# Reordering the end of the first attention and the shared expert's third group in a two-layer gated cross-attention and mixture kernel

## The chip, the cores and the metric

The kernel runs on one core of one Trainium2 chip. The metric is the device time in microseconds (us) of one execution. PE is the matmul engine (TensorE), PEld its weight loads, DVE the vector engine, ACT the scalar engine, POOL the GpSimd engine and SP the engine that issues most transfers. "SPq" and "ACTq" are transfers issued from those engines' queues.

## The reference

The input `x` is 16 batches of 128 rows by 256. Four layers follow one another, each added to `x` through a tanh gate:

```python
x = x + tanh(g_xattn[0]) * L0_xattn(layernorm(x), ctx)   # 16 heads, projections Wq Wk Wv Wo
x = x + tanh(g_ffn[0])   * L0_ffn(layernorm(x))          # 32 routed experts, top 4, CAP 128, and a shared expert
x = x + tanh(g_xattn[1]) * L1_xattn(layernorm(x), ctx, ctx)   # 8 heads
x = x + tanh(g_ffn[1])   * L1_ffn(layernorm(x))          # 8 experts, top 2, and a shared expert

# L0_ffn: sigmoid scores, the 4 best of 8 groups of experts, the 4 best experts in them
routed = sum over the 4 experts of weight * down(relu(up(x))**2)
shared = relu(x @ shared_up.T)**2 @ shared_down.T        # hidden width 512
```

The change touches the end of `L0_xattn`, all of `L0_ffn`, and the start of `L1_xattn`.

## The kernel before, in words

The whole of `x` stays on the chip as the tile `X`. Each engine has one program, written out by hand, in which the order of the work is the order of the code; an engine that waits on a semaphore holds back all that is behind it in its program. Semaphore waits are written `w.wait_ge(semaphore, value)`.

**Attention.** `attention_pe` (L401 on), `attention_dve` (L555 on), `attention_act`, `attention_pool` (L240 on) and `attention_sp` (L183 on) each run steps `t`. Within a step the first layer counts heads `k` from 0 to 15 (on ACT `m` from 0 to 7, by pairs of heads). At step `t` batch `t` is in its exponentials, batch `t - 2` in its denominators and output, and so on, so the steps 16, 17 and 18 (`NB`, `NB + 1`, `NB + 2`) only drain the last batches. In a drained step, what is left on PE for batch b is: `denominators` (L512, at k == 12 of step b + 2), then on DVE `normalized` (L626, k == 13), then on PE `output` (L519, k == 15), then on ACT the scaling into `rd` (L355, first thing in step b + 3), then on POOL the addition to `X` (L276). For the last batch, 15, this happens in steps 17 and 18. Each engine's program calls a `meanwhile` hook at each k or m, behind the attention's own work of that k. By it the first feed-forward layer is started inside the attention's last steps.

**Start of the first feed-forward layer.** On DVE: per group of four batches the row statistics (`rows`, L1197; `statistics`, L1204 and L1207), on POOL the inverse roots (`roots`, L778), on DVE the normalized values `XN` (`normed_rows`, L1212). On PE: pairs of batches are transposed (`transposed`, L823), copied out as columns (on DVE L1232, the last ones on ACT L991), multiplied with the gate's weights into rows of logits for a group of four batches (`logit_rows`, L833), copied out (DVE L1236 or ACT L996), and transposed back (`logits`, L842). ACT takes sigmoids of eight batches at a time (`sigmoids`, L1000). `marks_dve` then finds the chosen experts for eight batches in a chain of small DVE instructions (L1088 to L1125), written as a generator, so that it can be run a piece at a time: its pieces are the sum with the bias (L1088), four maxima and minima (L1091 to L1094), three more (L1096 to L1098), two (L1100, L1101), the comparisons (L1104, L1106, L1108, L1110, one piece each), and the rest (L1112 to L1125). It runs once for batches 0 to 7 and once for 8 to 15.

**Between.** `ffn0_pe` runs the shared expert in 16 chunks `hidden` (L880; chunk n is up projection c = n mod 4 of group n // 4) and four groups `down` (L892). ACT follows with `relu_squared` (L975, L977) and `copied_out` (L1023). In between DVE counts places (`route_dve`, L1138 to L1187) and PE sums a table of token indices (`table`, L923, four parts, each after its DVE comparison L1173). When the table is read (L1177, L1178), POOL issues the 32 gathers of rows for the routed experts (L800, one indirect transfer per expert).

**Routed experts.** For expert x, PE transposes the gathered rows (L946), multiplies expert x - 1 up (L957) and x - 2 down (L965); ACT copies (L1051, L1056), DVE squares (L1315) and scales (L1321). SP stores each result to `ye` (L759) and reloads weights for the last experts (L762).

**Behind them.** `ffn0_pe_later` runs the last four chunks `hidden` and the last `down`. `ffn0_act_later` does the same on ACT; its last two `copied_out` stand in step t = -4, m == 2, of the second attention, ahead of the three QS transfers that ACT issues at m == 3 (L162). The second attention's five programs start behind a barrier (`all_done`, `stage`) to which each engine adds one. The operands of attention scores sit in four stacks of the tile `QS`. Each stack of the second attention needs a load of keys (L180) and two transfers of constant rows (`holes`, L2167). Stacks of batches 2 and 3 lie where the shared expert's input columns `XT0` are, so they can only be filled after the last `hidden`. In the kernel before SP does so at the end of `ffn0_sp`, ahead of the barrier, and PE waits for them there. POOL gathers the expert results (L297, 64 transfers, 4 per batch) in a fixed number per step, DVE adds them (`gathered`, L598 to L602), and POOL's root for a batch (L280) stands between two runs of gathers. DVE maxima of scores are L589, PE scores L425.

`shared_added` (L1291) adds four batches of the shared expert's result to X: groups 0 and 1 before the experts, group 2 at expert 16, group 3 in step 1 of the second attention.

Of the kernel before, what the change touches and what calls it, by code (L numbers as in the profile page):

```python
# [21 lines left out]
U = 4  # L22
# [37 lines left out]
class Layer:  # L60


    def __init__(self, name, H, R, sem, before=None, gathers=None, keys=None, kept=None):
# [44 lines left out]
        self.s0 = 0 if self.first else 2  # L108

# [73 lines left out]
def attention_sp(e, w, A, M, loads, behind_first=None):  # L183
# [4 lines left out]
    for t in A.steps():  # L188
# [20 lines left out]
        if within(b1):  # L209
            if not A.first and b1 >= U:  # L210

                w.wait_ge(A.st, A.NP * (b1 - U + 1))
                keys_loaded(e, A, M, b1)
            w.wait_ge(A.res2, b1 + 1)
            w.wait_ge(A.st, A.NP * (b1 - U + 1))
            for k in range(3 if b1 == 0 else 6):
                spread(e, A, M, b1, k)
                if k == 2 and within(b5) and A.first:
                    reciprocals()
            if b1 == 0 and behind_first:  # L220
                behind_first()
        elif within(b5) and not A.late(b5):
            reciprocals()
# [181 lines left out]
def attention_pe(e, w, A, M, meanwhile=lambda t, k: None):  # L405
# [71 lines left out]
    def keys_of(b):  # L477
        w.wait_ge(A.ldc[b % U], 16 * ((A.n0 + b) // U + 1))
# [253 lines left out]

def ffn0_sp(e, w, G, A, B, M, d):
# [14 lines left out]
    def stack_ready(b):  # L748

        for k in range(2):  # L750
            w.wait_ge(B.kept[k], 96 * NB // 2)
        w.wait_ge(B.kept[2], 32)
        keys_loaded(e, B, M, b)
        for got in holes(e, M, d, B.stack(b), second=True):
            got.then_inc(G.late, 16)

    for x in range(E0):
        w.wait_ge(G.ey, x + 1)
        e.dma_start(M["ye_d"][CAP * x:CAP * x + CAP, :], M["YE"][x % 4]).then_inc(G.sty[x % 4], 16)  # L759
        if x + PLACES < E0:  # L760
            w.wait_ge(G.ed, x + 1)
            e.dma_start(M["EW"][x], M["ew_d"][x + PLACES, :, :]).then_inc(G.again[x], 16)  # L762

        if x in (PLACES - 4, PLACES):
            w.wait_ge(G.ed, x)
            stack_ready((x - PLACES + 4) // 4)

    w.wait_ge(G.up, 4 * NGRP)
    for b in (2, 3):
        stack_ready(b)  # L770
# [4 lines left out]
def ffn0_pool_meanwhile(e, w, G, M):  # L775
    def roots(g):
        w.wait_ge(G.bn, 3 * g + 3)
        e.tensor_tensor(M["frs"][:, GB * g:GB * g + GB], M["fve"][:, GB * g:GB * g + GB], M["mhalf4"][:, :],  # L778
                        ALU.pow).then_inc(G.rs, 1)

    def at(t):
        if t == NB - 2:
            roots(0)
            roots(1)
        if t == NB - 1:
            roots(2)
        if t == NB + 2:
            roots(3)

    return at  # L790
# [15 lines left out]
def ffn0_pe_meanwhile(e, w, G, A, M):  # L806
# [20 lines left out]
    def logit_rows(g):  # L827
        w.wait_ge(G.xt, 2 * g + 2)
        w.wait_ge(G.lc, g)
        if g == 3:  # L830
            w.wait_ge(A.exp, A.NP * NB)
        for a in range(2):
            got = e.matmul(BK[5 if g == 3 else 1][0:E0, :], M["GW"][:, a, :], XT[:, a, 512 * g:512 * g + 512],  # L833
                           start=(a == 0), stop=(a == 1))
# [62 lines left out]
def ffn0_pe_later(e, w, G, M):  # L897

    w.wait_ge(G.er, E0)
    hidden(e, w, G, M, 12, 13, 14, 15)  # L900
    w.wait_ge(G.ey, E0)
    down(e, w, G, M, 3)
    w.wait_ge(G.xs, NB)
    w.wait_ge(G.late, 16 * (PLACES - EARLY + 2 * U))


def ffn0_pe(e, w, G, A, M):
# [30 lines left out]
    down(e, w, G, M, 2)  # L938
    w.wait_ge(M["w_e"], 16 * EARLY)
    w.wait_ge(G.late, 16 * (PLACES - EARLY))  # L940
    for x in range(E0 + 2):
# [19 lines left out]
        if 0 <= y < E0:  # L961
            w.wait_ge(G.es, y + 1)
            w.wait_ge(G.xs, NB - GB)
# [21 lines left out]
def ffn0_act_meanwhile(e, w, G, A, M):  # L985
# [17 lines left out]
    def at(t, m):  # L1003
        if t == NB + 1 and m == 0:
            sigmoids(0, 2)
        if t == NB + 2 and m == 7:
# [19 lines left out]
def ffn0_act_later(e, w, G, M):  # L1026

    relu_squared(e, w, G, M, 12, 13, 14, 15)
# [9 lines left out]
def ffn0_act(e, w, G, M):  # L1038
# [7 lines left out]
    copied_out(e, w, G, M, 8, 12)  # L1046
# [144 lines left out]
def ffn0_dve_meanwhile(e, w, G, A, M, step):  # L1191
# [8 lines left out]
    def statistics(g, last):  # L1200
        last.then_inc(G.bn, 1)
        w.wait_ge(G.bn, 3 * g + 1)
        for b in range(GB * g, GB * g + GB):
            got = e.bn_aggr(mv[:, b, :], M["f6"][:, b, :])  # L1204
        got.then_inc(G.bn, 1)
        w.wait_ge(G.bn, 3 * g + 2)
        e.tensor_scalar(M["fve"][:, GB * g:GB * g + GB], mv[:, GB * g:GB * g + GB, 1], EPS, None, ALU.add).then_inc(G.bn, 1)  # L1207

    def normed_rows(g):
        w.wait_ge(G.rs, g + 1)  # L1210
        for b in range(GB * g, GB * g + GB):
# [22 lines left out]
    def logit_rows(g):  # L1234
        w.wait_ge(G.lr, g + 1)
        e.tensor_copy(M["LR"][g % 2], M["BK"][1][0:E0, :]).then_inc(G.lc, 1)  # L1236
# [7 lines left out]
    def at(t, k):  # L1244
# [22 lines left out]
        if t == NB and k == 14:  # L1267
            logit_rows(0)
        if t == NB + 1:
            if k == 0:  # L1270
                logit_rows(1)
                columns(4, 5)
            if k == 15:
                rows(12, 15)
                marks(1)
        if t == NB + 2 and k == 15:
            statistics(3, rows(15, 16))
            marks(1)
            normed_rows(3)
            for _ in first:  # L1280
# [13 lines left out]
def ffn0_dve_later(e, w, G, M):  # L1294
    def at(t, k):
        if t == 1 and k == 6:
# [5 lines left out]
def ffn0_dve(e, w, G, A, M, step):  # L1302
# [6 lines left out]
    for x in range(E0 + 1):  # L1309
        if x == E0 // 2:  # L1310
            shared_added(e, w, G, M, 2)
# [55 lines left out]
SHARED = ((0, 128), (128, 128), (256, 96))  # L1367

# [802 lines left out]
def build(nc, d, out):  # L2171
    with ExitStack() as ctx:
# [42 lines left out]
        def sp_program(e):  # L2215
# [23 lines left out]
            attention_sp(e, w, L1, M, lambda e, w, n: rows(n))  # L2239
# [154 lines left out]
```

## Time and profile before

| what | value |
|---|---|
| median of 3 runs | 773.63 us (771.66 to 774.16) |
| the profiled execution, its own time | 771.27 us |
| its span in the trace | 769.5 us |
| busy, share of the span | PE 87%, PEld 45%, DVE 68%, ACT 48%, POOL 45% |
| mean granted TensorE clock | 0.959 |
| first attention ends, about | 264 us (last addition to X) |
| routed experts | 317 to 372 us |
| second attention's first scores | 394 us |

Times in the rows are us from the start of the span. A timeline row is: start, duration, engine, line, operation, output and inputs, shapes, count, and in brackets the idle time before it with what ended it. Rows with "x4" merge several instructions. An f32 matmul is two instructions in these rows. Matmul ends are modelled.

### The profile page before, as it was taken

Reading aid. Unit: us, or ns where it says so; the run is one execution under the profiler, and the core shown is the slowest. Engines: PE = TensorE matmul, PEld = TensorE weight load, DVE = VectorE, ACT = ScalarE, POOL = GpSimd, SP = SyncE. Lnnn points to the kernel's source line nnn. Section 1 sums busy time; section 2 is a strip of 40 time slices with the busy share of each in tenths; the row PEclk is TensorE's granted clock in tenths of the full one; section 3 lists DMA queues with packets and bytes.
Section 4 is the critical chain, followed back from the end, with each engine's and each line's share of the span. In section 5 each row is a group of like instructions: output and inputs, shape, how many; then the busy total and the mean of one; then the engine's idle time right before and its main releaser. Section 6 shows DMA issues by size and latency. Waiting matters only on the chain.

```text
span 769.5 us, 13735 instructions
## 1 busy us (share of the span) xinstructions
PE 668.0 (87%) x4737; PEld 347.7 (45%) x4738; DVE 523.1 (68%) x1248; ACT 368.9 (48%) x612; POOL 343.6 (45%) x401
## 2 busy tenths in 40 slices
PE   3889999999999999778845699999887999897996
PEld 1233333333333356667512344445332566565763
DVE  3788888898887599435267799998636832332336
ACT  2057777877778354234413566666402213333420
POOL 3836465564412100655367887520100067666530
PEclk9999999999999999979966999999969999999999
DMA  6945454565522660245644778877511022222137
GB/s 157 196 114 138 129 141 131 158 179 151 156 65 67 200 179 14 67 122 149 209 128 127 206 217 236 221 197 194 161 46 29 0 68 81 73 67 74 49 94 265
DMA packets 111708, 101.12 MB, mean 131 GB/s; under 512 B 26517, under 2 KB 95802, under 8 KB 111512
## 3 DMA queue, kind: packets, MB, share of 16 engines
q1 hardware_dynamic: 99872, 76.19, 35.4%
q0 software_dynamic: 8352, 18.74, 8.6%
q10 hardware_dynamic: 3416, 5.31, 2.8%
q8 instruction: 38, 0.62, 0.4%
q14 instruction: 30, 0.25, 0.1%
HBM read 58.49 MB, written 24.40 MB: 108 GB/s over the span
## 4 chain that ended last, share of the span: by engine, by line
PE 54%; DVE 17%; issue 9%; POOL 6%; DMA 5%; SPq 4%; another core or an unknown queue 2%; ACT 2%; ACTq 0%; POOLq 0%; DVEq 0%
PE S L425 9%; PE O L470 9%; PE ST L1537 5%; DVE mx L589 5%; POOL spare L297 3%; PE ST L433 3%; PE ST L1463 2%; PE M L1554 2%; PE S L1554 2%; PE M L519 2%; PE ST L957 2%; PE M L512 2%; SPq L174 2%; DMA QS<-mxT 1%
## 5 line engine op out<-in xcount | busy, mean ns | idle before, releaser
L589 DVE TENSOR_REDUCE mx<-S 128x2 f32<-128x512 f32 x384 | 250.9, 684 | 34.8 <-PE S L425 33.1
L345 ACT ACTIVATE PX<-ST 128x1024 f32<-128x1024 f32 x192 | 196.2, 1024 | 92.0 <-PE ST L433 84.6
L425 PE MATMUL S<-QS 62*128 62x256 bf16 (+1 forms) x768 | 150.7, 292 | 39.5 <-DVE mx L589 26.0
L433 PE MATMUL ST<-QS 64*128 64x256 bf16 (+1 forms) x768 | 140.0, 276 | 1.4 <-DMA QS<-mxT 1.1
L470 PE MATMUL O<-PX,VA 128*32 128x256 f32 x1536 | 122.3, 391 | 0.3 <-DMA VA<-in_val 0.2
L425 PEld LDWEIGHTS S<-QS 62*128 62x128 bf16 (+1 forms) x768 | 47.7, 97 | 157.4 <-DVE mx L589 95.3
L297 POOL DMA_INDIRECT spare<-ye,GI x64 | 67.7, 1058 | 29.1 <-DMA ye<-QKc 14.8
L1648 POOL DMA_INDIRECT PX<-xn,TI x39 | 39.9, 1022 | 63.6 <-DVE K1n L1837 39.7
L800 POOL DMA_INDIRECT PX<-xn,TI x32 | 34.5, 1077 | 58.7 <-DVE spare L1186 44.1
L433 PEld LDWEIGHTS ST<-QS 64*128 64x128 bf16 (+1 forms) x768 | 53.3, 96 | 16.1 <-issue 9.0
L1537 PE MATMUL ST<-EGU,Cb 128*128 x156 | 54.7, 474 | 4.7 <-issue 2.9
L1655 POOL DMA_INDIRECT yt<-QKc,DI x39 | 39.3, 1008 | 24.5 <-ACT QKc L1617 17.0
L276 POOL TENSOR_TENSOR X<-X,rd 128x256 f32<-128x256 f32 x16 | 11.6, 727 | 86.2 <-ACT rd L355 81.2
L470 PEld LDWEIGHTS O<-PX,VA 128*32 128x32 f32 x1536 | 30.4, 108 | 41.1 <-issue 39.1
L280 POOL TENSOR_TENSOR rs<-ve,mhalf 128x1 f32<-128x1 f32 x32 | 18.1, 565 | 50.7 <-DVE ve L581 50.0
L1537 PEld LDWEIGHTS ST<-EGU,Cb 128*128 128x128 f32 x156 | 27.1, 193 | 15.1 <-issue 7.0
L308 POOL TENSOR_TENSOR QKc<-QKc,QKs 128x512 f32<-128x512 f32 (+1 forms) x29 | 27.0, 929 | 13.5 <-ACT QKs L394 10.9
L1965 DVE TENSOR_TENSOR rd<-ST,rd 128x176 f32<-128x176 f32 x19 | 6.5, 342 | 37.8 <-ACT rd L1610 21.3
L1965 DVE TENSOR_TENSOR Xn<-ST,Xn 128x176 f32<-128x176 f32 x20 | 6.8, 342 | 35.7 <-ACT Xn L1610 28.5
L337 ACT ACTIVATE OS<-O 128x512 f32<-128x512 f32 x48 | 28.1, 585 | 2.3 <-DMA rd<-OS 1.9
L317 POOL TENSOR_TENSOR QKs<-QKc,QKs 128x512 bf16<-128x512 f32 (+1 forms) x29 | 27.4, 947 | 3.2 <-ACT QKs L397 1.6
L880 PE MATMUL ST<-QS,SU 128*128 128x512 f32 x64 | 28.7, 598 | 0.1
(302 smaller groups left out, 1127.3 us busy)
## 6 DMA issues: line engine op xcount, KB each, us to landing
QS<-QKs SPq DMA_DIRECT2D x93, 128.0 KB
QS<-keys SPq DMA_DIRECT2D x16, 512.0 KB
keys<-spare SPq DMA_DIRECT2D x96, 64.0 KB
QS<-QKs SPq DMA_DIRECT2D x93, 64.0 KB
EGU<-in_ew SPq DMA_DIRECT2D x16, 256.0 KB, 2.7
xn<-spare SPq DMA_DIRECT2D x8, 512.0 KB, 5.7
ye<-QKc SPq DMA_DIRECT2D x32, 128.0 KB
VA<-in_val SPq DMA_DIRECT2D x16, 256.0 KB
```

Of the source, the lines that this page charges most:

```text
L297: e.indirect_dma_start(out=M["GA"][b7 % 3][:, T * k:T * k + T], out_offset=None, in_=M["ye_d"], in_offset=bass.IndirectOffsetOnAxis(ap=M[" ...
L345: e.activation(M["PX"][pair % 4][:, :], M["ST"][pair % 2][:, :], ACT.Exp, scale=A.scale).then_inc(A.exp, 1)
L425: got = e.matmul(M["S"][n % 2][:, 256 * a:256 * a + 256], QS[:, 0, 128 * a:128 * a + 128], QS[:, 1, :], start=True, stop=True)
L433: got = e.matmul(M["ST"][(NP * t + k // 2) % 2][:, 512 * u + 256 * a:512 * u + 256 * a + 256], QS[:, 1, 128 * a:128 * a + 128], QS[:, 0, : ...
L470: got = e.matmul(M["O"][32 * u:32 * u + 32, 256 * (quad % 2):256 * (quad % 2) + 256], V[:, a, 4 * quad + u, :], M["PX"][pair % 4][:, 512 * ...
L589: e.tensor_reduce(M["mx"][b % 2][:, :, A.row_of_max(head)], M["S"][n % 2][:, :].rearrange("p (a s) -> p a s", a=2), AX.X, ALU.max, negate= ...
L800: e.indirect_dma_start(out=M["GX"][x % GATHERS], out_offset=None, in_=M["xn_d"], in_offset=bass.IndirectOffsetOnAxis(ap=M["TI"][:, x:x + 1 ...
L880: got = e.matmul(M["BK"][3 + n % 2], M["SU"][:, a, 128 * c:128 * c + 128], M["XT0"][:, a, 512 * g:512 * g + 512], start=(a == 0), stop=(a ...
L1537: got = e.matmul(BK[3 + 2 * (j % 2)][:, 0:2 * I1], M["XeT1"][j % 2][:, 128 * a:128 * a + 128], M["EGU"][:, bass.ds(expert[j], 1), a, :], s ...
L1554: got = e.matmul(BK[1 if j % 2 else 7][:, 0:T], M["HT1"][j % 2][0:HALF, 128 * a:128 * a + 128], M["ED"][:, bass.ds(expert[j], 1), a, :], s ...
L1648: e.indirect_dma_start(out=M["XE1"][i % TILES], out_offset=None, in_=M["xn1_d"], in_offset=bass.IndirectOffsetOnAxis(ap=M["TI1"][:, i:i + ...
L1655: e.indirect_dma_start(out=M["yt_d"], out_offset=bass.IndirectOffsetOnAxis(ap=M["DI1"][:, j:j + 1], axis=0), in_=M["YE"][j % 4][:, :], in_ ...
```

## The change

On all five engines the steps 16 to 18 of the first attention are refilled, groups for the normalization become 4, 4, 4, 2, 2 batches (table `NORMS`), the third `down` goes from before the routed experts to behind them, and the last stacks of keys are loaded by SP behind the second attention's second spread (`b1 == 1`) where they were ahead of the barrier. PE's wait for them moves to the scores that use them (`holes`).

```diff
+        self.holes = 0 if self.first else 32
...
-            if b1 == 0 and behind_first:
+            if b1 == (0 if A.first else 1) and behind_first:
                 behind_first()
...
     def keys_of(b):
-        w.wait_ge(A.ldc[b % U], 16 * ((A.n0 + b) // U + 1))
+        w.wait_ge(A.ldc[b % U], 16 * ((A.n0 + b) // U + 1) + A.holes)
...
         if x in (PLACES - 4, PLACES):
             w.wait_ge(G.ed, x)
-            stack_ready((x - PLACES + 4) // 4)
-
-    w.wait_ge(G.up, 4 * NGRP)
-    for b in (2, 3):
-        stack_ready(b)
+            stack_ready(e, w, B, M, d, (x - PLACES + 4) // 4)
...
+        if t == NB + 1:
+            roots(3)
         if t == NB + 2:
-            roots(3)
+            roots(4)
...
+        if g % 2:
             w.wait_ge(A.exp, A.NP * NB)
         for a in range(2):
-            got = e.matmul(BK[5 if g == 3 else 1][0:E0, :], M["GW"][:, a, :], XT[:, a, 512 * g:512 * g + 512],
+            got = e.matmul(BK[5 if g % 2 else 1][0:E0, :], M["GW"][:, a, :], XT[:, a, 512 * g:512 * g + 512],
...
         if t == NB:
+            if k == 3:
+                logit_rows(0)
             if k == 12:
-                logit_rows(0)
+                logit_rows(1)
             if k == 15:
-                logit_rows(1)
                 logits(0)
+                logits(1)
                 transposed(4)
         if t == NB + 1:
             if k == 1:
-                logits(1)
                 transposed(5)
+            if k == 3:
+                logit_rows(2)
+            if k == 13:
+                hidden(e, w, G, M, 0)
             if k == 15:
-                logit_rows(2)
-                hidden(e, w, G, M, 0, 1)
+                transposed(6)
+                hidden(e, w, G, M, 1)
         if t == NB + 2 and k == 15:
-            transposed(6, 7)
+            transposed(7)
             logit_rows(3)
...
 def ffn0_pe_later(e, w, G, M):
     w.wait_ge(G.er, E0)
-    hidden(e, w, G, M, 12, 13, 14, 15)
+    hidden(e, w, G, M, 12, 13)
     w.wait_ge(G.ey, E0)
+    down(e, w, G, M, 2)
+    hidden(e, w, G, M, 14, 15)
     down(e, w, G, M, 3)
     w.wait_ge(G.xs, NB)
-    w.wait_ge(G.late, 16 * (PLACES - EARLY + 2 * U))
...
     for q in range(4):
         table(q)
-    down(e, w, G, M, 2)
...
+        if t == NB + 1 and m == 7:
             logit_rows(2)
             relu_squared(e, w, G, M, 0)
-            columns(6, 7)
+        if t == NB + 2 and m == 7:
+            columns(6)
             relu_squared(e, w, G, M, 1)
+            columns(7)
             logit_rows(3)
...
 def ffn0_act_later(e, w, G, M):
-    relu_squared(e, w, G, M, 12, 13, 14, 15)
+    relu_squared(e, w, G, M, 12, 13)
+    copied_out(e, w, G, M, 8, 12)
+    relu_squared(e, w, G, M, 14, 15)
     copied_out(e, w, G, M, 12, 14)
...
-        if t == NB and k == 14:
-            logit_rows(0)
+        if t == NB:
+            if k == 12:
+                logit_rows(0)
+            if k == 14:
+                logit_rows(1)
         if t == NB + 1:
-            if k == 0:
-                logit_rows(1)
+            if k == 1:
                 columns(4, 5)
+            if k == 2:
+                marks(4)
+            if k == 14:
+                statistics(3, rows(12, 14))
+                marks(1)
             if k == 15:
-                rows(12, 15)
+                rows(14, 15)
                 marks(1)
         if t == NB + 2 and k == 15:
-            statistics(3, rows(15, 16))
-            marks(1)
             normed_rows(3)
+            statistics(4, rows(15, 16))
+            marks(2)
+            normed_rows(4)
...
 def ffn0_dve_later(e, w, G, M):
     def at(t, k):
+        if t == -1 and k == 3:
+            shared_added(e, w, G, M, 2)
         if t == 1 and k == 6:
             shared_added(e, w, G, M, 3)
...
-        if x == E0 // 2:
-            shared_added(e, w, G, M, 2)
...
+NORMS = ((0, 4), (4, 8), (8, 12), (12, 14), (14, 16))
...
+            def columns_left():
+                w.wait_ge(X.up, 4 * NGRP)
+                for b in (2, 3):
+                    stack_ready(e, w, L1, M, d, b)
+
+            attention_sp(e, w, L1, M, lambda e, w, n: rows(n), columns_left)
```

## Rows read from the trace of the kernel before

**Rows 1.** Windows 262 to 267 us: busy of PE, PEld, DVE, ACT, POOL, then granted clock, DMA share, GB/s

```profile
262.00:267.00 5.00, 4.71 (x8) 1.38 (x9) 3.26 (x15) 1.06 (x2) 1.61 (x2) 0.66 1.02 334
```

**Rows 2.** Timeline of PE at the first attention's end

```profile
256.81 1.88 PE L833 MATMUL S<-QS,GW 128*32 128x512 f32 x4 [0.23 <-DVE QKc L1236]
...
260.42 0.66 PE L823 MATMUL S<-ident,spare 128*128 128x128 f32 x4 [0.42 <-DVE QS L1232]
...
261.00 0.69 PE L512 MATMUL M<-rT,hbL 16*128 16x256 f32 x2
...
262.29 1.19 PE L519 MATMUL M<-on,Wo 128*128 128x256 f32 x2 [0.59 <-DVE on L626]
...
263.41 3.06 PE L833 MATMUL S<-QS,GW 128*32 128x512 f32 x4
...
274.65 7.13 PE L880 MATMUL ST<-QS,SU 128*128 128x512 f32 x16
```

**Rows 3.** Timeline of DVE, same stretch

```profile
259.67 0.69 DVE L1232 COPY QS<-S 128x512 f32<-128x512 f32 x1 [0.27 <-PE S L823]
...
264.99 0.43 DVE L1197 BATCH_NORM_STATS2 f<-X 128x6 f32<-128x256 f32 x1 [1.45 <-POOL X L276]
...
267.39 1.38 DVE L1212 TENSOR_SCALAR spare<-X,fmv,frs 128x256 f32<-128x256 f32 x4 [0.61 <-POOL frs L778]
...
277.10 0.43 DVE L1088 TENSOR_TENSOR spare<-spare,bc 128x256 f32<-128x256 f32 x1
```

**Rows 4.** Timeline of ACT, same stretch

```profile
263.52 0.56 ACT L355 ACTIVATE rd<-M,bog,tg 128x256 f32<-128x256 f32 x1 [3.10 <-PE M L519]
...
269.04 0.63 ACT L977 ACTIVATE RL<-RL 128x512 f32<-128x512 f32 x1
...
274.76 0.38 ACT L1000 ACTIVATE spare<-ST 128x256 f32<-128x256 f32 x1 [0.52 <-PE ST L842]
```

**Rows 5.** Timeline of PE, the last quarter of the table

```profile
309.20 0.64 PE L923 MATMUL M<-OS,PX 128*128 128x64 bf16 x16 [1.13 <-DVE PX L1173]
```

**Rows 6.** Timeline of POOL: the second gather for the routed experts

```profile
312.97 1.92 POOL L800 DMA_INDIRECT PX<-xn,TI  x1 [0.31 <-issue]
```

**Rows 7.** Transfers, 310 to 320 us: GB/s in 40 slices of 0.25 us

```profile
GB/s 0 0 0 0 0 0 0 0 0 0 0 0 0 2 0 0 0 0 0 0 0 0 221 129 240 0 0 2 0 0 0 0 98 37 0 0 0 1 10 0
```

**Rows 8.** Timeline of PE, the end of the third down and the first expert

```profile
315.80 1.03 PE L892 MATMUL O<-SD,Cb 128*128 128x256 f32 x4
...
316.67 0.60 PE L946 MATMUL S<-ident,PX 128*128 128x128 f32 x4
```

**Rows 9.** The chain that ended last, 318 to 375 us: start, us, what

```profile
322.39 2.86 another core or an unknown queue
```

**Rows 10.** Timeline of PE behind the routed experts

```profile
372.21 7.13 PE L880 MATMUL ST<-QS,SU 128*128 128x512 f32 x16
...
380.78 1.97 PE L892 MATMUL ST<-SD,RL 128*128 128x256 f32 x8 [1.44 <-issue]
...
386.04 1.89 PE L892 MATMUL O<-SD,RL 128*128 128x256 f32 x8
...
393.95 1.01 PE L425 MATMUL S<-QS 126*128 126x256 bf16 x4 [6.03 <-DMA QS<-QKs]
```

**Rows 11.** Timeline of ACT behind the routed experts

```profile
384.51 0.47 ACT L1023 ACTIVATE spare<-O,tg 128x256 f32<-128x256 f32 x1 [1.25 <-PE O L892]
...
387.82 0.42 ACT L394 ACTIVATE QKs<-QKc 128x256 bf16<-128x256 f32 x1 [2.84 <-issue]
...
390.09 1.87 ACTq L162 DMA_DIRECT2D QS<-QKs  x3
```

**Rows 12.** Timelines of SP, DVE and POOL behind the routed experts

```profile
381.53 1.12 SPq L2167 DMA_DIRECT2D QS<-in_hole  x2
...
384.15 0.69 DVE L598 TENSOR_TENSOR spare<-spare 128x512 f32<-128x512 f32 x1 [11.53 <-issue]
...
399.81 0.56 POOL L280 TENSOR_TENSOR rs<-ve,mhalf 128x1 f32<-128x1 f32 x1 [2.25 <-DVE ve L581]
```

More of the change, by code:

```diff
@@ L730, in up_chunk, with stack_ready @@
     return n // 4, n % 4
+def stack_ready(e, w, B, M, d, b):
+    for k in range(2):
+        w.wait_ge(B.kept[k], 96 * NB // 2)
+    w.wait_ge(B.kept[2], 32)
+    keys_loaded(e, B, M, b)
+    for got in holes(e, M, d, B.stack(b), second=True):
+        got.then_inc(B.ldc[b % U], 16)
 def ffn0_sp(e, w, G, A, B, M, d):
@@ L746, in ffn0_sp @@
     e.dma_start(rows[:, :, T:ROW0], M["wd"]).then_inc(G.wrow, 16)
[L748 to L755, printed above, removed]
     for x in range(E0):
@@ L775, in ffn0_pool_meanwhile, with roots @@
 def ffn0_pool_meanwhile(e, w, G, M):
[L776 to L779, printed above, removed]
+    def roots(n):
+        lo, hi = NORMS[n]
+        w.wait_ge(G.bn, 3 * n + 3)
+        e.tensor_tensor(M["frs"][:, lo:hi], M["fve"][:, lo:hi], M["mhalf4"][:, 0:hi - lo], ALU.pow).then_inc(G.rs, 1)
     def at(t):
@@ L829, in logit_rows @@
         w.wait_ge(G.lc, g)
-        if g == 3:
+        if g % 2:
             w.wait_ge(A.exp, A.NP * NB)
         for a in range(2):
-            got = e.matmul(BK[5 if g == 3 else 1][0:E0, :], M["GW"][:, a, :], XT[:, a, 512 * g:512 * g + 512],
+            got = e.matmul(BK[5 if g % 2 else 1][0:E0, :], M["GW"][:, a, :], XT[:, a, 512 * g:512 * g + 512],
                            start=(a == 0), stop=(a == 1))
@@ L962, in ffn0_pe @@
             w.wait_ge(G.es, y + 1)
-            w.wait_ge(G.xs, NB - GB)
+            w.wait_ge(G.xs, NB - 2 * GB)
             w.wait_ge(G.ey, y - 1)
@@ L1005, in at @@
             sigmoids(0, 2)
-        if t == NB + 2 and m == 7:
+        if t == NB + 1 and m == 7:
             logit_rows(2)
             relu_squared(e, w, G, M, 0)
-            columns(6, 7)
+        if t == NB + 2 and m == 7:
+            columns(6)
             relu_squared(e, w, G, M, 1)
+            columns(7)
             logit_rows(3)
@@ L1045, in ffn0_act @@
     relu_squared(e, w, G, M, 10, 11)
-    copied_out(e, w, G, M, 8, 12)
     for x in range(E0 + 1):
@@ L1198, in rows, with statistics, normed_rows @@
         return got
-    def statistics(g, last):
+    def statistics(n, last):
+        lo, hi = NORMS[n]
         last.then_inc(G.bn, 1)
-        w.wait_ge(G.bn, 3 * g + 1)
-        for b in range(GB * g, GB * g + GB):
+        w.wait_ge(G.bn, 3 * n + 1)
+        for b in range(lo, hi):
             got = e.bn_aggr(mv[:, b, :], M["f6"][:, b, :])
         got.then_inc(G.bn, 1)
[L1206 to L1211, printed above, removed]
+        w.wait_ge(G.bn, 3 * n + 2)
+        e.tensor_scalar(M["fve"][:, lo:hi], mv[:, lo:hi, 1], EPS, None, ALU.add).then_inc(G.bn, 1)
+    def normed_rows(n):
+        w.wait_ge(G.rs, n + 1)
+        for b in range(*NORMS[n]):
             e.tensor_scalar(M["XN"][:, b, :], M["X"][:, b, :], mv[:, b, 0:1], M["frs"][:, b:b + 1],
@@ L1235, in logit_rows @@
         w.wait_ge(G.lr, g + 1)
-        e.tensor_copy(M["LR"][g % 2], M["BK"][1][0:E0, :]).then_inc(G.lc, 1)
+        e.tensor_copy(M["LR"][g % 2], M["BK"][5 if g % 2 else 1][0:E0, :]).then_inc(G.lc, 1)
     first = marks_dve(e, w, G, M, step, 0, 8)
@@ L2238, in sp_program @@
             rows = ffn1_sp_meanwhile(e, w, G1, M)
-            attention_sp(e, w, L1, M, lambda e, w, n: rows(n))
+            def columns_left():
[3 more added lines that the diff above has]
+            attention_sp(e, w, L1, M, lambda e, w, n: rows(n), columns_left)
             ffn1_sp(e, w, G1, M, o_out)
```

## The prediction

> **What bounds the kernel now.** I read the windows first, then the timelines of the engines over three stretches, then the chain that ended last. In the first stretch, 252 to 310 us, the chain goes from the last batch's output matmul on PE [rows 2] over its scaling on ACT [rows 4], the addition on POOL and the statistics on DVE (264.99 us) to the normalized values (267.39 us), and from there through DVE alone: the first marks, the second marks (from 277.10 us) [rows 3], the routing, up to the last quarter of the table, for which PE has waited 1.13 us [rows 5]. PE is thus only 1.13 us behind being the bound. In the second stretch, the experts, it is PE and ACT passing work on, with waits that the chain puts down to an unknown queue; the first is 2.86 us [rows 9] and the chain has four of them between 322.39 and 332.45 us. In the third, behind the experts, the chain runs over POOL's gathers, but each of POOL's roots has waited for DVE's statistics (2.25 us at 399.81 us) [rows 12], and DVE had to wait for the operands of the first scores, with PE, until 393.95 us [rows 10]. The reader is to see that DVE, not POOL's issue, sets the pace there.
>
> **The change, part by part.** Sums are made in the profiled execution (771.27 us, its span 769.5 us); it stands 2.36 us under the median of 773.63 us, and I add that at the end.
>
> **First logits earlier.** A row of logits is 1.88 us on PE [rows 2], copies on DVE 0.69 us [rows 3]. The first starts behind the last value matmuls at 253.5 us, its copy ends at 256.1 us, the second ends at 258.0 us. Then come output 14 (0.65), two sets of logits (0.36 each, the second behind its copy) and a pair's transposes (0.6 us, [rows 2]) up to 259.9 us. Copy, transposes, copy bring the columns of batches 8 to 11 at 262.0 us. Where the old PE program ran the last batch's denominators at 261.00 us [rows 2], the new one first runs the third row of logits, at full clock until 263.9 us. Denominators at 263.9 us, then `hidden(0)` (1.78 us, a fourth of 7.13 [rows 10]), then the output at 266.3 us, against 262.29 us [rows 2]. The old output took 1.19 us at a low clock; taking 0.65 us, it ends at 267.0 us.
>
> **Four marks ahead.** They are 0.45 + 0.85 + 0.77 + 0.5 = 2.6 us of DVE and fit where DVE would wait for the denominators, 262.0 to 264.6 us. They cost nothing as long as PE has that row of logits to run; without this cover they would delay the normalized values by 2.6 us.
>
> **The scaling.** ACT now has `relu_squared(0)` in front of the last scaling: relu and square, 0.63 us each [rows 4]. The scaling starts at 267.65 us against 263.52 us, and the last statistics at 269.1 us against 264.99 us: 4.1 us later.
>
> **What is given back.** Behind them DVE has two batches to aggregate and norm instead of four (0.7 for 1.38 us [rows 3]), the root on POOL lies under two marks, and all comparisons of the first marks are done. 269.1 + 0.45 statistics + 0.45 aggregation + 1.45 marks + 0.7 + 4.2 for the remaining marks gives 276.3 us. But the second marks wait for the second sigmoid: from the normalized values at 272.1 us transposes 0.6, columns 0.65, logits 1.88, copy 0.6, logits 0.36, sigmoid 0.4 with hand-overs lead to 276.8 us. Against 277.10 us [rows 3] DVE gains 0.3 us. PE starts `hidden(2)` at 276.35 us against 274.65 us [rows 2], 1.7 us later; of these 1.13 us vanish in its wait before the table [rows 5]. So the table, and with it all gathers, come **0.6 us later**; I keep 0 to 1 us with no change of clock.
>
> **The third down, taken out before the experts.** It is four times 1.73 us of PE, 6.9 us (from 380.78 to 386.04 us three of four [rows 10]). What hid it is the gathers: the second one was issued for 1.92 us from 312.97 us [rows 6], and its data moved from 315.5 to 316.25 us [rows 7], while PE came out of its down at 316.67 us [rows 8]. The second expert's transposes stand in front of the first up projection, so the loop can start only 0.4 us earlier. With gathers 0.6 us later the two cancel. Bounds: every later expert could be up to 1.2 us ahead, as the small gathers land about that much before they are used; and nothing is gained if the waits on the unknown queue [rows 9] have fixed ends. I take 0.2 us later, with 1.2 us earlier to 0.6 us later as bounds. The addition taken from DVE in the loop, 1.2 us, stood before a wait for a later expert, so it brings 0; at most 0.8 us, by which that expert was late. Put into step -1 it lies in a wait for a gather.
>
> **The third down, put behind them.** PE then has 6.9 us more before it starts the second attention. The `down`s are in order, so ACT's copy at 384.51 us [rows 11] comes at 391.4 us, and the ACT program has this copy in front of its first cast of the second attention: 387.82 us [rows 11] becomes 391.9 us, 4.1 us later. The last `down` ends at 387.93 + 6.9 = 394.85 us [rows 10]. The last two copies stand, on ACT, in front of the three QS transfers of batch 0. These go out at 395.4 us instead of 390.09 us [rows 11]; the first scores start at 399.3 us instead of 393.95 us [rows 10], **5.3 us later**. Queued behind on DVE are three maxima, the additions of batch 2 and its statistics; for these POOL's root waits (399.81 us [rows 12]), and behind it the next gathers. All move by 5.3 us. The lower bound is 4.1 us, should only the cast count; it is less only if POOL's schedule takes it up (a rival).
>
> **The key loads, moved.** SP ended them at 382.65 us, then took part in the barrier, and DVE started at 384.15 us with no transfer named as its releaser [rows 12]. Without them DVE can start about 2 us earlier, at gather speed; but ACT's cast at 391.9 us comes later than all of that. Price 0, bound -2 us. Behind the second spread they cost SP 3.3 us of issue, in front of a transfer for which SP waited 10 us: 0. The higher values in PE's waits cost nothing. The added transfers beside the gathers are a rival below.
>
> **Sum.** 0.2 + 5.3 = 5.5 us: 776.8 us in this execution, **779.1 us** as a median.
>
> **Rivals.**
>
> *Clock (0.15).* In 262 to 267 us the granted clock was 0.66 [rows 1], in part the level 1.2 GHz, after gaps of PE, and the row of logits took 3.06 instead of 1.88 us [rows 2]. If the new third row, the denominators and `hidden(0)` fall in such a stretch, 2.4 us are added in front of the output: 781.5 us. The new order has more and larger gaps from 258.6 to 262.0 us, about 1.4 of 3.4 us; against it, the old drop came before a dense stretch too. The Trainium skill ("TensorE: Matmul & The Clock Gate", Part 1) says that the throttled state is the default and activity releases it; by that rule, more gaps ahead of the row speak for this rival.
>
> *Keys beside gathers (0.12).* 1.3 MB for two stacks now move while POOL's gathers of batch 3 are under way, at 404 to 409 us. If these land 2 us later, DVE's additions and all behind do: 781 us. For it: between 381 and 383 us, while they ran, the 16 engines moved 342 GB/s and were full. Against it: the gathers there were in time. The Trainium skill ("DMA: Bandwidth & Descriptors", "Issuing engines are not separate DMA queues") says that SP's and POOL's transfers interleave on the same 16 engines, which supports it.
>
> *POOL takes it up (0.14, faster).* POOL needs 64 x 1.3 = 83 us for its gathers. If its issue sets the pace of the second attention's start, the roots' waits (2.25 us [rows 12] and four others) shrink, and the 5.3 us vanish there; the earlier barrier brings 2 us and the loop 1 us, less 0.6: 771.2 us. It decides if scores of batch 0 start no later than 396 us, or POOL shows no wait for them. Against it: in all five cases POOL was the one that waited.
>
> *The experts' waits shrink (0.17, no change).* Four waits of 9.4 us in sum hang on something that I can't name [rows 9]. With ACT and PE free at the loop's start they may fall by about half, 4.7 us: 774.4 us.
>
> *Forecast (0.42).* Its own range is 777 to 781 us.
>
> **How the numbers follow.** A measurement of this kernel can tell 0.3% (2.3 us) from no change, so the bounds are 771.3 and 775.95 us. Slower: forecast, clock and keys, 0.69. Same: the shrunk waits, 0.17. Faster: 0.14. The range goes from 773.5 us, inside the case of no change, to 783 us, which holds clock and keys with 1.5 us of spread.
>
> **What would show it.** Right: the last output matmul at 266 to 267 us, marks L1088 to L1101 in front of L626; second marks within 1 us of 277 us; no wait before the last quarter of the table; first expert within 1 us of 316.7 us; L880 and L892 in turn behind the experts up to 395 us; ACT's first cast near 392 us; the first L425 of the second attention near 399 us; POOL's root of batch 2 near 405 us. Wrong: first scores before 396 us, or the experts ending before 370 us.

## The result, and the profile after

In 20 runs each the kernel before took 769.97 us and the changed one 775.81 us, a ratio of **1.0092 [1.007, 1.0114]** (95% interval): slower. The medians lie 5.8 us apart, the ratio is worth 7.1 us (5.4 to 8.8). The two profiled executions differ by only 2.0 us (773.24 against 771.27), so places are compared in the traces and times by the ratio. The page of the changed kernel, its span and the shares of the chain that ended last:

```profile
span 771.4 us, 13739 instructions
...
PE 61%; DVE 12%; issue 9%; POOL 6%; DMA 4%; SPq 3%; ACT 2%; another core or an unknown queue 2%; ACTq 0%; POOLq 0%; DVEq 0%
```

In the chain of the kernel before PE had 54% and DVE 17%. In what follows, "cast" is ACT's L394 (L396 in the changed kernel), which turns a normalized batch of the second attention into bf16; the transfers of its operands (QS) go out behind it, and the first scores wait for them. "Root n" is POOL's root for batch n of the second attention.

**The first attention's end.** The timeline of PE in the changed kernel answers to [rows 2, 5]:

```profile
262.47 1.90 PE L834 MATMUL S<-QS,GW 128*32 128x512 f32 x4 [0.79 <-DVE QS L1243]
264.31 0.69 PE L514 MATMUL M<-rT,hbL 16*128 16x256 f32 x2
264.93 1.98 PE L887 MATMUL ST<-QS,SU 128*128 128x512 f32 x4
266.75 0.59 PE L521 MATMUL M<-on,Wo 128*128 128x256 f32 x2
...
276.65 7.13 PE L887 MATMUL ST<-QS,SU 128*128 128x512 f32 x16
...
308.51 2.03 PE L931 MATMUL M<-OS,PX 128*128 128x64 bf16 x64
```

Third row of logits, denominators, `hidden(0)` and last output stand in the order forecast; denominators and output start 0.4 and 0.45 us behind their forecast (263.9 and 266.3 us). The 64 products of the table now come in one piece: the 1.13 us of [rows 5] are gone. DVE's second marks answer to [rows 3]:

```profile
277.25 0.42 DVE L1098 TENSOR_TENSOR spare<-spare,bc 128x256 f32<-128x256 f32 x1 [0.62 <-ACT spare L1007]
```

277.25 against 277.10 us, and now it is the second sigmoid that they wait for, as forecast.

**The start of the experts.** PE's timeline answers to [rows 8]; the windows below it show the granted clock (third number from the right):

```profile
314.63 0.66 PE L953 MATMUL S<-ident,PX 128*128 128x128 f32 x2 [4.08 <-DMA PX<-xn,TI]
317.44 0.69 PE L953 MATMUL S<-ident,PX 128*128 128x128 f32 x2 [2.16 <-DMA PX<-xn,TI]
317.92 1.06 PE L964 MATMUL ST<-on,EGU 128*128 128x128 f32 x4
```

```profile
310.00:314.00 4.00, 0.54 (x19) 0.42 (x15) 3.14 (x10) 0.00 (x0) 1.61 (x2) 0.86 0.00 0
314.00:318.00 4.00, 1.22 (x5) 0.85 (x6) 0.70 (x1) 0.38 (x1) 3.39 (x3) 0.50 0.15 37
318.00:322.00 4.00, 4.00 (x19) 3.71 (x19) 1.07 (x3) 1.70 (x5) 3.08 (x4) 0.50 0.05 9
```

This I had not foreseen. Without the third down PE was busy for 1.76 of the 8 us from 310 to 318 us, the clock fell to 0.50 (1.2 GHz), and until 323 us each group of products of the up projection took 1.06 us instead of 0.61 to 0.71 us. The experts end at 374.1 us against 372.1 us.

**Behind the experts.** PE (answers to [rows 10]) and ACT (to [rows 11]):

```profile
384.66 3.60 PE L887 MATMUL ST<-QS,SU 128*128 128x512 f32 x8
389.60 1.99 PE L899 MATMUL ST<-SD,RL 128*128 128x256 f32 x8 [1.35 <-ACT RL L984]
...
394.88 1.89 PE L899 MATMUL O<-SD,RL 128*128 128x256 f32 x8
400.37 0.60 PE L427 MATMUL S<-QS 126*128 126x256 bf16 x4 [3.60 <-DMA QS<-QKs]
```

```profile
393.36 0.47 ACT L1032 ACTIVATE spare<-O,tg 128x256 f32<-128x256 f32 x1 [1.25 <-PE O L899]
393.73 0.41 ACT L396 ACTIVATE QKs<-QKc 128x256 bf16<-128x256 f32 x1
...
396.81 0.47 ACT L1032 ACTIVATE spare<-O,tg 128x256 f32<-128x256 f32 x1 [1.25 <-PE O L899]
396.82 1.87 ACTq L164 DMA_DIRECT2D QS<-QKs  x3
```

The cast stands directly behind the copy of the second of four downs, the three transfers directly behind the last copy; a cast that was ready earlier waited in ACT's program. DVE had the first batch normalized at 388.61 us (388.14 + 0.47), so the cast came 5.1 us after it could have; DVE's wait, 5.56 us, also holds the cast itself. Further on DVE waits for the gathers of batch 3 (timeline of DVE, the same row of the kernel before, then SP and POOL; to [rows 12]):

```profile
394.17 0.43 DVE L613 TENSOR_TENSOR QKc<-QKc,QKs 128x256 f32<-128x256 f32 x1 [5.56 <-ACT QKs L396]
...
412.82 0.69 DVE L600 TENSOR_TENSOR spare<-spare 128x512 f32<-128x512 f32 x1 [5.03 <-DMA spare<-ye,GI]
```

```profile
404.75 0.69 DVE L598 TENSOR_TENSOR spare<-spare 128x512 f32<-128x512 f32 x1 [2.91 <-DMA spare<-ye,GI]
```

```profile
404.40 0.59 SPq L182 DMA_DIRECT2D QS<-keys  x1
...
406.85 1.12 SPq L2189 DMA_DIRECT2D QS<-in_hole  x2
```

```profile
405.76 0.56 POOL L282 TENSOR_TENSOR rs<-ve,mhalf 128x1 f32<-128x1 f32 x1 [2.60 <-DVE ve L583]
406.50 1.05 POOL L299 DMA_INDIRECT spare<-ye,GI  x1 [0.18 <-issue]
407.85 1.00 POOL L299 DMA_INDIRECT spare<-ye,GI  x1 [0.30 <-issue]
...
415.86 0.56 POOL L282 TENSOR_TENSOR rs<-ve,mhalf 128x1 f32<-128x1 f32 x1 [3.24 <-DVE ve L583]
```

Root of batch 2 is 5.95 us behind 399.81 us [rows 12], that of batch 3 7.7 us behind its old place:

```profile
408.14 0.56 POOL L280 TENSOR_TENSOR rs<-ve,mhalf 128x1 f32<-128x1 f32 x1 [0.99 <-DVE ve L581]
```

The second pair of key loads went out beside the last two gathers of batch 3.

Root 15 is 8.5 us later in this pair (521.9 against 513.4 us), yet the spans differ by 1.9 us: from root 15 to the end the kernel before takes 256.1 us and the changed one 249.5 us, where nothing was changed. The twelve later profiles take 237.3 to 240.7 us there. So this pair's 2.0 us are no measure of the change, only the ratio is.

### The profile page after: what moved, and what is told of

Same layout as the page of the kernel before. It is cut to its first block, busy times and chain, and to the rows that moved or that the text cites. A ratio compares the mean times of both kernels' runs of the same rounds, so it can differ in the third digit from the quotient of the medians.

```text
span 771.4 us, 13739 instructions
## 1 busy us (share of the span) xinstructions
PE 667.1 (86%) x4738; PEld 350.6 (45%) x4738; DVE 523.9 (68%) x1249; ACT 368.7 (48%) x612; POOL 342.1 (44%) x402
## 4 chain that ended last, share of the span: by engine, by line
PE 61%; DVE 12%; issue 9%; POOL 6%; DMA 4%; SPq 3%; ACT 2%; another core or an unknown queue 2%; ACTq 0%; POOLq 0%; DVEq 0%
PE O L472 10%; PE S L427 10%; PE ST L1559 6%; DVE mx L591 5%; POOL spare L299 4%; PE ST L887 2%; PE ST L1485 2%; PE ST L435 2%; PE M L1576 2%; PE S L1576 2%; SPq L164 2%; PE M L521 2%; PE ST L964 2%; PE M L514 2%
## 5 line engine op out<-in xcount | busy, mean ns | idle before, releaser
L472 PEld LDWEIGHTS O<-PX,VA 128*32 128x32 f32 x1536 | 30.6, 108 | 41.9 <-issue 39.8
L310 POOL TENSOR_TENSOR QKc<-QKc,QKs 128x512 f32<-128x512 f32 (+1 forms) x29 | 27.0, 931 | 14.6 <-ACT QKs L396 12.6
```

Source lines behind the costliest of these rows:

```text
L472: got = e.matmul(M["O"][32 * u:32 * u + 32, 256 * (quad % 2):256 * (quad % 2) + 256], V[:, a, 4 * quad + u, :], M["PX"][pair % 4][:, 512 * ...
```

## The experiments

My theory was that the loss sits in ACT's order behind the experts; the rivals were the refill, the key loads beside the gathers, the clock at the loop's start, and PE's own time. In the three comparisons that follow the kernel before took 742.6 to 744.6 us, not 769.97; ratios are against the runs of before in the same comparison.

**One part at a time.** e1 has the diff's hunks for `ffn0_pe_meanwhile`, `ffn0_act_meanwhile`, the roots and DVE's statistics and marks alone. e2 has all the others. e3 has only the moved loads, e4 only the moved down, with ACT's copies and DVE's addition of it:

```
 e3: ffn0_sp            -    w.wait_ge(G.up, 4 * NGRP)
                        -    for b in (2, 3): stack_ready(b)
     attention_sp       +    behind_first() once b1 == 1
 e4: ffn0_pe            -    down(e, w, G, M, 2)
     ffn0_pe_later      +    down(e, w, G, M, 2)  between hidden(12, 13) and hidden(14, 15)
 e2: e3 and e4
```

> The kernel before with only the first attention's end changed (four marks ahead, the last group normed in two halves, the third row of logits and hidden(0) ahead of the last output). Theory: this part is worth 0.3 to 0.7 us, since the 4 us by which the last output comes later are given back at the second marks; ratio to the kernel before 1.000 to 1.001, second marks within 0.5 us of where the changed kernel has them (277.25 us), first expert at or before 317 us and no half-clock experts, since the third down still fills PE there. Rival (the whole loss lies in the refill, by way of a later table): ratio 1.007 or more.

> The kernel before with the third shared result behind the routed experts and the key loads behind the spread, the first attention's end as before. Theory: it has the whole loss, ratio 1.006 to 1.009 (+4.6 to +7 us), experts ending about 2 us later, first scores of the second attention about 6 us later. Rival (refill): ratio within 0.002 of one.

> The kernel before with the loads of keys and holes for two stacks behind the spread of the first batch, all else as before. Theory: the experts end as before; the additions behind them start about 2 us earlier, ACT's cast and the first scores with them (392 us for 393.95), but the transfers meet the gathers of batch 3, which costs about 2 us there: ratio 0.997 to 1.001. Rival (these transfers are what makes the changed kernel slower): ratio 1.004 or more, with POOL's root of batch 3 more than 2 us later relative to its root of batch 2.

> The kernel before with the third shared result behind the routed experts, while the loads of keys and holes keep their place ahead of the barrier. They wait for the 16th up projection, which now comes behind that down, near 388 us. Theory: the barrier, the additions and ACT's cast come near 392 to 394 us, later than in the changed kernel, the first scores near 401 us: ratio 1.008 to 1.013, more than with the loads moved. Rival (what costs is the loads beside the gathers, the down is free): ratio 1.003 or less.

Measured: e1 1.0027 [1.0002, 1.0052], e2 1.0079 [1.0049, 1.011], e3 1.0014 [0.9984, 1.0043], e4 1.0105 [1.0051, 1.0159]. The loss is in the moved down; the loads cost little by themselves, and leaving them ahead of the barrier (e4) is no cheaper. The ratios of e2 and e4 lie in their ranges, that of e3 0.0004 above its own. In e2 the experts did not end 2 us later, and the scores came 4.5 to 4.8 us later for the 6 expected (both by the table further on).

e1 missed its range and its places: DVE's second marks at 278.85 us and PE's first transposes for an expert at 318.97 us. Its PE timeline says why (`hidden(1)` and the last row of logits):

```profile
269.98 3.49 PE L888 MATMUL ST<-QS,SU 128*128 128x512 f32 x4
273.31 0.60 PE L825 MATMUL S<-ident,spare 128*128 128x128 f32 x4
275.31 1.90 PE L835 MATMUL ST<-QS,GW 128*32 128x512 f32 x4 [1.40 <-ACT QS L999]
```

3.49 us for what took 1.88 us in the changed kernel's profile: the clock was 0.60 over 270 to 274 us, behind a stretch in which PE had waited for the normalized values. So DVE's second marks waited 2.27 us for the sigmoid.

**The order on ACT, and the clock.** e5 puts ACT's copies behind the transfers, e6 fills the gap, e7 does both:

```
 e5: ffn0_act_later     -    copied_out(e, w, G, M, 12, 14)
                        -        if t == -4 and m == 2: copied_out(e, w, G, M, 14, 16)
                        +        if t == -4 and m == 3: copied_out(e, w, G, M, 12, 16)
 e6: ffn0_pe            +    8 matmuls BK[2] <- RLs, SD behind table(3), 4 more ahead of x == 1
```

> The changed kernel with ACT's last four copies (12 to 15) put behind its first cast, second cast and three transfers of the second attention, instead of in front of them. Theory: in the changed kernel the normalized batch 0 has waited over 5 us in ACT's queue behind the copies, so the cast comes about 4 us earlier; the first scores then wait only for the end of the last down, about 3 to 3.5 us earlier than in the changed kernel; ratio to the kernel before 1.003 to 1.007, against 1.009 for the changed kernel. Rival (PE's own 6.9 us more of down set it): no change of the first scores by over 1 us, ratio 1.008 or more.

> The changed kernel with 12 matmuls of 128x256 whose results nobody reads where the third down stood before: 8 behind the table, 4 between the first two experts' transposes, on a bank that is free. Theory: TensorE's clock fell in that gap (0.50 to 0.54 granted), so the first experts ran at half speed; with the filler it is 1.00 and the experts end 1.5 to 2.5 us earlier; ratio to the kernel before 1.005 to 1.008. Rival (the gathers' landing sets the end of the experts, whatever the clock): the clock is up but the experts end as before, ratio 1.009 or more.

> Both of the last two edits in the changed kernel. Theory: the two costs add, so about 5 us come back against the changed kernel, what is left is 1 to 2 us of the first attention's end and 1 to 2 us of the loads beside the gathers: ratio 1.001 to 1.005. Rival (costs hidden behind each other): no better than the better one of the two.

Measured: 1.0124 [1.0093, 1.0154], 1.01 [1.0061, 1.0139], 1.0115 [1.0083, 1.0147]: all above my ranges and in the ratios of the rivals. The changed kernel was not run in this comparison; its ratio was 1.0092 before and is 1.0108 in e9. With six runs each and intervals of 0.003 to 0.004 to each side, a gain of 2.4 us (0.0032) can't be told here. The places tell more. In e5 the first scores came 2.4 us earlier, which is neither my 3 to 3.5 us nor the rival's nothing. In e7 the cast and the transfers are where I wanted them, and the first scores stand 0.57 us behind PE's last down, a wait for ACT's copy of it (ACT, then PE):

```profile
378.16 0.40 ACT L396 ACTIVATE QKs<-QKc 128x256 bf16<-128x256 f32 x1
...
379.99 1.90 ACTq L164 DMA_DIRECT2D QS<-QKs  x3
```

```profile
382.46 1.99 PE L899 MATMUL ST<-SD,RL 128*128 128x256 f32 x8 [0.44 <-ACT spare L1044]
384.30 1.89 PE L899 MATMUL O<-SD,RL 128*128 128x256 f32 x8
386.75 0.61 PE L427 MATMUL S<-QS 126*128 126x256 bf16 x4 [0.57 <-ACT spare L1044]
```

The mended order freed 2.4 us and no more; then PE's 6.9 us are the bound, with two waits for ACT's late copies (0.44 and 0.57 us), and batch 1's cast waits behind ACT's last copy in place of batch 0's. The clock in e6 was 1.00 from 302 to 334 us, without a measurable gain in time.

**The loads split.** e8 is e3 with batch 3's loads one spread later than batch 2's and ACT's copies 14 and 15 behind the transfers. e10 is the changed kernel with the edits of e5 and the split, e11 the same without the new first attention's end; e9 is the changed kernel again, for this comparison:

```
 attention_sp           -    if b1 == (0 if A.first else 1) and behind_first: behind_first()
                        +    if b1 in ((0,) if A.first else (1, 2)) and behind_first: behind_first(b1)
 columns_left(b1)       +    stack_ready(e, w, L1, M, d, b1 + 1)
```

> The kernel before with the loads of keys and holes moved as in the change, but the fourth batch's one spread later than the third's, and ACT's last two copies behind its three transfers. Theory: with the loads moved as in the change the ratio was 1.0014, as 2 us gained at the barrier were given back where the loads met the gathers of batch 3; halving that collision brings about 1 us and the transfers go out 0.5 to 0.9 us earlier: ratio 0.997 to 1.000. Rival (what delays those gathers is their place in POOL's program, not the loads): ratio 1.001 to 1.002.

> The changed kernel itself, beside the others on the same chip, since a first-attention part of 1.0027 and a rest of 1.0079 add up to more than the 1.0092 measured before. Theory (the parts add): ratio 1.009 to 1.012. Rival (on a chip without waits on an unknown queue among the experts the change costs less): 1.005 to 1.008.

> The changed kernel with ACT's copies 12 to 15 behind its three transfers and the fourth batch's loads of keys and holes one spread later. Theory: with the order mended alone the scores came 2.4 us earlier, and POOL's root of batch 3 only 1, since the loads met the gathers of batch 3; with the loads split, root 3 stands near 38 us behind the end of the experts (41 in the changed kernel), ratio 0.002 to 0.004 below that of the changed kernel beside it. Rival: what comes earlier at the start of the second attention is lost again on its way, ratio within 0.002 of it.

> The same two edits, with the first attention's end as before the change. Theory: what is left of the cost is PE's 6.9 us behind the experts, some 3 us at the first scores, less what the second attention takes up: ratio 1.003 to 1.006. Rival (PE's time there is free once the order is mended): within 0.002 of one.

Measured: e8 0.9993 [0.9964, 1.0021], e9 1.0108 [1.0074, 1.0143], e10 1.0051 [1.0018, 1.0083], e11 1.006 [1.0029, 1.0092]. The parts add, as e9's theory had it: 1.0027 and 1.0079 make 1.0106. The gather's wait, one row of DVE's timeline from e3, e8, e5 and e10:

```profile
395.43 0.69 DVE L600 TENSOR_TENSOR spare<-spare 128x512 f32<-128x512 f32 x1 [4.97 <-DMA spare<-ye,GI]
```

```profile
396.13 0.69 DVE L600 TENSOR_TENSOR spare<-spare 128x512 f32<-128x512 f32 x1 [2.93 <-DMA spare<-ye,GI]
```

```profile
405.38 0.69 DVE L600 TENSOR_TENSOR spare<-spare 128x512 f32<-128x512 f32 x1 [5.01 <-DMA spare<-ye,GI]
```

```profile
400.06 0.69 DVE L600 TENSOR_TENSOR spare<-spare 128x512 f32<-128x512 f32 x1 [2.90 <-DMA spare<-ye,GI]
```

e5 and e10 differ in nothing but the split of the loads, so two microseconds of that wait are the loads, as the prediction's rival "keys beside gathers" had it; e8's rival (the place in POOL's program) is out. e10 (750.02 us) and e11 (749.76 us) win back about half of the loss of e9 (753.85 us), though the intervals still touch, and stay slower than before (744.63 us); e10's gain on e9, 0.0057, is more than the 0.002 to 0.004 that I expected, while root 3 at 38.6 us is where I expected it. e8 and e11 came into their ranges. No version beat the kernel before by more than can be measured.

**PE's time alone.** e12 is the kernel before with 16 matmuls of a down's shape put in front of `hidden(12, ...)`, and nothing removed:

> The kernel before with 16 matmuls of 128x256 (6.9 us of PE, the size of one down, results read by nobody) put in right behind the experts, and nothing taken out anywhere. Theory: taking the down out before the experts brought nothing, so this costs what the moved down costs: experts end as before, first scores 4 to 5.5 us later relative to them, ratio 1.006 to 1.009. Rival (the loop's start did gain, and the moved down costs more than that): ratio 1.010 or more.

Measured 1.0103 [1.0051, 1.0155]. Its experts ended at 360.8 us and its PE went (first filler, last down, first scores):

```profile
361.11 1.10 PE L904 MATMUL ST<-SD,RL 128*128 128x256 f32 x4 [0.26 <-issue]
...
381.82 1.89 PE L892 MATMUL O<-SD,RL 128*128 128x256 f32 x8
388.84 1.01 PE L425 MATMUL S<-QS 126*128 126x256 bf16 x4 [5.14 <-DMA QS<-QKs]
```

Adding 6.9 us behind the experts costs as much as moving them there (e4: 1.0105). So the same 6.9 us had cost little or nothing where they stood before; both intervals are 0.005 wide to each side, 4 us, and the places say it more closely (table to experts' end 51.8 and 52.2 us). The ratio and the scores, 6.2 to 6.5 us later for 4 to 5.5 expected, are above my range, and by its ratio alone the rival would have won; that the loop's start had gained is what the places speak against. In e4 and e12 the last `hidden` also holds back the key loads, and with them the barrier and the cast (21.6 and 21.7 us in the table), so they price the 6.9 us on that path, not on the one of the changed kernel.

**All profiles side by side.** Each number is a start minus the end of the last expert's product on PE (for before 371.41 + 0.70 = 372.1 us), in us; the last column runs from the end of the table to that end.

| kernel | ACT's first cast | first scores | root 2 | root 3 | root 15 | table to experts' end |
|---|---|---|---|---|---|---|
| before | 15.7 | 21.8 | 27.7 | 36.0 | 141.3 | 62.3 |
| changed | 19.6 | 26.3 | 31.6 | 41.8 | 147.8 | 63.6 |
| e1 refill | 15.3 | 21.5 | 27.3 | 35.6 | 140.1 | 51.3 |
| e3 loads | 14.5 | 20.6 | 26.3 | 36.3 | 143.9 | 52.5 |
| e8 loads split | 14.4 | 20.8 | 26.3 | 34.6 | 143.0 | 53.7 |
| e4 down | 21.6 | 27.7 | 33.2 | 41.4 | 150.3 | 52.2 |
| e2 down, loads | 19.6 | 26.3 | 31.7 | 41.7 | 150.0 | 52.9 |
| e9 changed | 19.6 | 26.3 | 31.9 | 41.7 | 147.8 | 54.8 |
| e6 filler | 19.6 | 26.3 | 31.9 | 41.4 | 147.9 | 52.6 |
| e5 ACT order | 15.3 | 23.9 | 30.3 | 40.3 | 145.2 | 53.9 |
| e7 both | 15.3 | 23.9 | 30.5 | 41.0 | 147.5 | 51.3 |
| e10 order, split | 15.4 | 23.9 | 30.3 | 38.6 | 145.2 | 52.5 |
| e11 as e10, old refill | 15.3 | 23.9 | 30.3 | 38.6 | 145.2 | 55.2 |
| e12 PE later | 21.7 | 28.0 | 33.7 | 41.9 | 147.1 | 51.8 |

Up to root 2 the columns repeat to some 0.4 us between kernels of the same order, up to root 3 to 0.7 us; after that single profiles scatter by a few us.

Whether the low clock at the experts' start cost anything is read on DVE: the start of its scaling of expert x's result (L1321 in the kernel before; x from 0), in us from the end of the table, in the twelve later profiles.

| profiles | x = 1 | x = 2 | x = 4 | x = 20 |
|---|---|---|---|---|
| with the down (e1, e3, e8, e12) | 11.1 to 11.2 | 12.2 to 12.3 | 15.7 | 36.1 to 36.5 |
| without (e2, e4, e5, e9, e10, e11) | 11.5 to 12.8 | 12.6 to 14.0 | 15.8 to 16.2 | 35.9 to 36.4 |
| filler (e6, e7) | 10.6 | 11.7 | 16.0 to 16.2 | 35.7 |

The half clock delays the first experts by up to 1.8 us. At x = 4 all but 0.5 us of it is gone and at x = 20 all: ahead of x = 4 PE waits 0.99 to 1.02 us for a gather in the kernels with the down, and those without it catch up.

The first attention can be read the same way, from the end of its last value matmuls to the end of the table. With the old order the seven profiles give 55.84 to 55.88 us six times, and 56.35 us for the kernel before. With the new order four (changed, e5, e6, e7) give 56.54 to 56.56 us and three (e1, e9, e10) 58.14 to 58.20 us. In these three the clock had fallen; in e9 the third row of logits had it:

```profile
262.18 3.48 PE L834 MATMUL S<-QS,GW 128*32 128x512 f32 x4 [0.78 <-DVE QS L1243]
```

The old order met a low clock as well (before, e2, e3, e4: 0.57 to 0.66 over 262 to 266 us), and its table came no later for it in three of these four (the kernel before itself is the one at 56.35 us). Before the last quarter of the table PE waited 1.38 to 1.39 us at full clock (e8, e11, e12) and 0.59 to 0.66 us in e2, e3 and e4, so that wait took the drop up.

## Why the prediction came out as it did

Direction and size were right: 5.5 us or 1.0071 forecast, 1.0092 or 7.1 us measured, 5.8 us between the medians. The main term, the down behind the experts, was right in its mechanism. That the sum came out as near is in part luck: that term was 0.5 to 0.9 us too large, the refill up to 2.3 us for 0.6, and the loads, at 0 in the sum, cost 2 us at batch 3 for 1 us at the cast. The median of 775.81 us lies in the range; that it is below 779.1 us comes from the kernel before, whose 20 runs have a median 3.7 us below the 773.63 us that I had started from.

- **Refill, 0.6 us: right, with the rival on top.** At full clock the table is 0.7 us later (56.55 against 55.86). The clock rival (0.15) was not an alternative to the forecast but something that came in three of seven profiles, for 1.6 us each (58.2 against 56.55; I had 2.4). The weighted mean, 1.4 us, agrees with 1.0027, 2.0 us [0.1, 3.9]. The Trainium skill ("TensorE: Matmul & The Clock Gate", Part 1) has the throttled state as the default, which activity releases; by that rule, more gaps are more risk. The traces do not bear that out: the number of drops is no larger with the new order (three of seven, four of seven before). What is new is that they fall where nothing covers them.
- **The down taken out, 0.2 us: an effect left out, and no price found for it.** I said "they cancel", with bounds of 1.2 us earlier to 0.6 us later, and costed the matmuls at nothing because the gathers hid them. The first up projection did start 0.33 to 0.45 us earlier behind the table (7.38 to 7.50 us without the down and the filler, 7.83 us with the down), for the 0.4 forecast. What I left out is that the matmuls kept the clock up as well. All seven profiles without them and without filler had a granted clock of 0.50 to 0.65 in one or two of the 4 us windows there, all others 1.00 up to 325 us. Table to experts' end is 53.6 us in the mean of e2, e4, e5, e9, e10 and e11, 52.3 us with the down (e1, e3, e8, e12), 52.0 us with filler (e6, e7). That looks like 1.2 us, but the groups overlap (51.3 to 55.2), and by the table of DVE's scalings there is no difference left at expert 20. It arises in the last eleven experts: the four latest ends, 53.7 to 55.2 us (e8, e5, e9, e11), belong to profiles in which the clock fell again (0.50 to 0.88 in windows of 4 us between 354 and 366 us), one of them with the down; it fell in e6 too, and in none of the other seven. PE waits for gathers in all twelve (the longest such wait behind the second expert is 1.1 to 3.1 us in each). So the clock at the loop's start is shown, and by expert 20 its price in these twelve is nothing; whether a later drop is made likelier by it no run shows. The 2.0 us by which the experts end later in the first pair are 0.7 us of table and 1.3 us that mix with the waits on the unknown queue.
- **The down put behind: right.** The cast came 4 us later (4.1 forecast, 19.6 against 15.3 to 15.7 in the table), the scores 4.4 to 4.8 us later (5.3; 26.3 against 21.8 and 21.5), root 2 near 405 us (405.76, with experts that ended 2 us later than forecast). What I had not seen is that two bounds lay close together: ACT's order for 2.4 us, and behind it PE's own time.
- **The loads, 0 us: two effects that nearly cancel.** They let the cast start about 1 us earlier (14.5 against 15.3 and 15.7) and delay the gathers of batch 3: from root 2 to root 3 it is 9.5 to 10.5 us in the seven kernels with the loads moved together (changed, e2, e3, e5, e6, e7, e9), and 8.2 to 8.4 us in the seven others. The price of the rival "keys beside gathers", 2 us, was right. The Trainium skill ("DMA: Bandwidth & Descriptors", "Issuing engines are not separate DMA queues") says that they interleave on the same 16 engines; by that rule the loads can hold up the gathers, and the traces agree with 5.01 against 2.90 us (e5, e10).
- **POOL takes it up: no.** Root 15, counted from the experts' end, is 6.5 us later in the changed kernel. **The experts' waits shrink:** in the first pair the waits on an unknown queue among the experts fell from 11.7 us (six pieces) to 7.5 us (three), yet the experts ended later; and where e9's profile has none, the change costs 1.0108. It wasn't what decided.

Open: e10 is 0.0073 below e5, 5.4 us, though in another comparison, but the places show 1.7 us (root 3, 40.3 against 38.6) and none at root 15 (145.2 in both); the rest is scatter or lies where I have not looked.

## What to carry to other kernels

Work that hides a wait may do a second job; here it kept TensorE's clock up, although the gathers behind it took up what that was worth. Ask of each block that is moved not only who waits where it arrives, but what the engine does in the hole. And when an engine's program has work of one stage in front of the first step of the next, mend that order before blaming the work, but expect that the next bound is near: here 2.4 of some 4.6 us. Follow a loss past the place where it starts, too: the low clock was plain to see, and by expert 20 nothing of it was left.

## What the runs showed of the hardware

The granted clock fell to 1.2 GHz in or behind stretches in which PE waited, and not in each profile at the same place: with one and the same PE program around the refill it fell at 262 us (e9, e10), at 270 us (e1) or not at all (four profiles). And the same kernel before took 769.97 us in one comparison and 742.6 to 744.6 us in three others. Table to experts' end was 62.3 us in the first and 51.3 to 55.2 us in the others' profiles, and the chains of the twelve kernels of the other comparisons have no wait on an unknown queue there; what queue that is, no run here shows.
